# Expert stage of a Mamba-style mixer plus mixture-of-experts kernel: second weight ring filled only at a change of expert, row requests at other places, last small slot moved to the end

## The chip, the cores and the metric

The kernel runs on one core of a Trainium2 chip. The metric is the device time of one execution in microseconds; the median of three runs of the kernel before is 1149.23 us (1145.25 to 1150.15).

## The reference

The input is 4 sequences of 1024 tokens with 256 features (4096 tokens in all). Two layers follow each other.

```
x = x + layernorm(mixer(layernorm(x)))        # linear, conv, silu, selective scan, gated output
x = x + layernorm(ffn(layernorm(x)))

ffn:  probs = softmax(xn @ router_w)          # 8 experts
      topv, topi = top_k(probs, 2);  topv = topv / sum(topv)
      out = sum over e of comb[:, e] * (silu(clip(xn @ gate_e)) * (xn @ up_e)) @ down_e
          + shared expert
```

Each token goes to two of eight experts, so 8192 pairs of token and expert are computed, each expert with an inner width of 1024. With the reference's inputs the experts 0 to 7 get 508, 642, 476, 216, 1329, 3379, 439 and 1203 tokens.

## The kernel before

The first stage computes the mixer and, as tokens become ready, the routing; it also splits the experts' weights into a high and a low part and stores them in DRAM (`w_split`, `w_s` in the code: per expert 8 chunks of 768 KB, of which 512 KB are gate and up, 256 KB are down). Tokens are scattered to DRAM by expert (`xs_scratch`). This part ends at about 462 us.

The second stage (`experts`, from line 1231) works through 40 **slots**. A pair slot is 256 tokens of one expert in 8 steps; a small slot ("single") is 128 tokens in 4 steps. There are 31 pairs and 9 singles. `single(n)` (L1671) says which slots are small: 4, 8, ..., 36. Slots 0 to 4 are written out, slots 5 to 36 are a loop of eight iterations of four slots (`LEAD`, `BODY`, `REPEATS`, L51), slots 37 to 39 are written out again. Which expert a slot has is data: tables `group_expert`, `group_row`, `group_code`, `group_change`, filled by short vector instructions (L1062 to L1111 for the pairs; `plan_singles`, L1113, for the singles, one piece after each step of slot 0). The expert with the most tokens (5) comes first, with 13 pairs; the other pairs follow by expert number: 2, 3, 2, 1, 5, 2 and the 3 that still fit for expert 7. Singles are ordered by expert number too; an expert has one where its tiles of 128 tokens aren't covered by its pairs, and what is left over of the nine is an empty slot of expert 7.

TensorE multiplies each step's weights in three passes (high by high, high by low, low by high), VectorE and ScalarE make the activation, and 3 steps later (`LAG`) TensorE does the down product of that step. After a slot's last down product VectorE scales the result (`copy_y`, L1573; it stands at step 3 of the next slot), and GpSimd adds it to DRAM with one indirect transfer per 128 tokens (`add_y`, L1374; L1381). The adds of slot n wait until those of slot n-1 have landed (L1378).

SyncE (`sync`, L1284) issues all loads in one queue, in order:

- the **main ring** (`load_chunk`, L1300): 8 chunks, each in two transfers (L1302, L1303), conditional on `group_change`: where a pair has the same expert as the pair before, the instruction is there but moves nothing. A chunk's place is free when the slot before has done its down product with it (L1323).
- the **second ring** for the singles (`load_single`, L1305): 8 transfers of 768 KB, conditional too. They stand between the chunks in turns 4k+2 and 4k+3; a flag says which of the two turns issues them (the first one, where its main ring isn't reloaded; else the second). They are issued for each of the nine singles.
- the **rows** of the next slot (`next_rows`, L1285): 256 or 128 tokens, in a pair's turn after chunk 1 (L1325). It waits until the slot before has been weighed by VectorE (`meta_ready`, L1290; `weigh`, L1580, step 2 of a slot), since the buffer is that slot's.

The rows of slot 2 are asked for by the first line of `others` (L1351), after SyncE has waited for all scattered tokens and for padding rows that it writes behind each expert's tokens (L454 to L462).

At the end all adds must have landed (L1362), the sums are loaded, normalised and stored.

Of the kernel before, what the change touches and what calls it, by code (L numbers as in the profile page):

```python
# [4 lines left out]
F32 = mybir.dt.float32  # L5
F32R = mybir.dt.float32r
I32 = mybir.dt.int32
# [5 lines left out]
P = 128  # L13
# [34 lines left out]
NS = E + 1  # L48
NP = ((T * K + E * (P - 1)) // P - NS) // GT
SLOTS = NP + NS  # L50
LEAD, BODY, REPEATS = 5, 4, 8  # L51
CW = 4 * P + D
# [7 lines left out]
X_AT, D_AT, R_AT = 48, 48, 0  # L60
H_AT, XNT_AT, FULL_AT = 146080, 162496, 219456
GUW = 2 * 4 * P
# [3 lines left out]
def mixer(nc, x, w_e, w_s, weights, full, consts, shared, xs_dram, x1_dram, acc_dram, fill, vec, ident,  # L66
# [3 lines left out]
    with ExitStack() as ctx:  # L70
# [73 lines left out]
        unused, expert_f, passed_f, row_f, starred = [decay[:, 1, (4 + i) * 48:(4 + i) * 48 + NP] for i in range(5)]  # L144
        singles_at = [XNT_AT + k * 8 * CW for k in range(5)] + [H_AT + k * 8 * CW for k in range(2)] + [FULL_AT]
        single_ring = [nc.alloc_sbuf_tensor_at(f"single_ring{f}", [P, 2 * CW], F32R, offset=at) for f, at in enumerate(singles_at)]
        banks = [ctx.enter_context(nc.psum_tensor(f"bank{i}", [P, HALF], F32)) for i in range(8)]
# [45 lines left out]
        def free(engine, what):  # L193
# [17 lines left out]
            elif what == "acc":  # L211
                engine.wait_ge(ends_cleared, 16 * (E + 2))
                for i in range(2):
# [16 lines left out]
        x1 = [by_tile(flat(v[:, :, :])[:, k * TC * D:(k + 1) * TC * D]) for v in (e_raw, e_high) for k in range(2)]  # L230
        homes = (gu_ring, d_ring, single_ring, quad(u_flat[:, R_AT:R_AT + 2 * GT * ROW]), quad(x_home[0]), quad(x_home[1]),
                 u_flat[:, R_AT + 2 * GT * ROW:R_AT + 2 * GT * ROW + DC * G].rearrange("p (c g) -> p c g", g=G),
# [127 lines left out]
        def _(sp):  # L360
            rows_of_star, weights_of_star, other_groups = e_sync(sp)

# [22 lines left out]
            def store_shared(k):  # L385
                for f in range(2):
                    rows = slice(k * HALF + f * 2 * P, k * HALF + (f + 1) * 2 * P)
                    sp.wait_ge(s_out, 2 * k + f + 1)
                    sp.dma_start(acc_dram[rows, :].rearrange("(t p) d -> p t d", p=P), sh_of(k)[f]).then_inc(s_stored[buf_of(k)][f], 16)
# [65 lines left out]
            for e in range(E):  # L455
                row = sp.value_load(end_row[0:1, e:e + 1], min_val=e * CAP, max_val=e * CAP + T)
                sp.dma_start(xs_dram[bass.ds(row, G), :].rearrange("(p m) d -> p (m d)", p=P), spare).then_inc(ends_cleared, 16)
            store_shared(2 * B - 1)
            sp.wait_ge(ends_cleared, 16 * (E + 2))
            for half in range(2):  # L460
                sp.wait_ge(scattered[half], B * 16 * HT * K)
            sp.wait_ge(plan_ready, 1)  # L462
            other_groups()
# [338 lines left out]
        def _(dve):  # L802
# [261 lines left out]
            def planned(i):  # L1064

                n[0] += 1
                i.then_inc(steps, 1)
                dve.wait_ge(steps, n[0])
# [25 lines left out]
            thirds = expert_f[:, 0:3 * NS].rearrange("p (i k) -> p i k", k=3)  # L1094
            nc.vector.tensor_tensor(group_change[:, NP:SLOTS], thirds[:, :, 2], thirds[:, :, 1], ALU.is_equal)

# [16 lines left out]
            def plan_singles(step):  # L1113
# [28 lines left out]
                if step == 6:  # L1142
                    nc.vector.tensor_copy(group_expert[:, NP:SLOTS], code)
                    nc.vector.tensor_scalar(group_code[:, NP:SLOTS], code, -1.0, float(E), ALU.mult, ALU.add)
                    planned(nc.vector.scalar_tensor_tensor(out=row, in0=number[:, 0:NS], scalar=float(P), in1=row,
                                                        op0=ALU.mult, op1=ALU.add))
                    planned(nc.vector.tensor_scalar(rest, number[:, 0:NS], float(-P), float(SPARE), ALU.mult, ALU.add))
                if step == 7:
                    planned(nc.vector.tensor_tensor(rest, rest, ended[:, :, E - 1], ALU.mult))
                    planned(nc.vector.tensor_tensor(row, row, rest, ALU.add))  # L1150
                    nc.vector.tensor_copy(group_row[:, NP:SLOTS], row).then_inc(plan_ready, 1)
# [79 lines left out]
def experts(nc, ctx, w_s, xs_dram, acc_dram, x1_dram, out, group_expert, group_change, group_row, group_code, vec, ident, neg_half,  # L1231
# [12 lines left out]
    by_chunk = lambda v: v.rearrange("p (m c k) -> p c m k", m=2, c=DC)  # L1244
    gus_hi, gus_lo = [[by_chunk(v[:, at:at + 4 * P]) for v in w_single] for at in (0, CW)]
    ds_hi, ds_lo = [[v[:, at + 4 * P:at + CW] for v in w_single] for at in (0, CW)]
    ids = sb("ids", [P, 2, GT], I32)
# [36 lines left out]
    def sync(sp):  # L1284
# [19 lines left out]

        def load_single(f, e, wanted):  # L1305
            sp.dma_start(w_single[f][:, :].bitcast(F32), w_s[e, f, :, :], cond=wanted).then_inc(single_loaded, 16)

        def turn(i, n):
            if single(n):
                if n + 1 < SLOTS:  # L1310
                    next_rows(i, n)
                return
            e = sp.value_load(group_expert[0:1, bass.ds(table_at(i, n), 1)], min_val=0, max_val=E - 1)
            new = sp.value_load(group_change[0:1, bass.ds(table_at(i, n), 1)], min_val=0, max_val=1)
            last = n - 2 if single(n - 1) else n - 1
            to_come = NP + before(i, n, ones_at)
            loads_single = n % BODY in (2, 3) and n + 3 < SLOTS
            if loads_single:
                e_single = sp.value_load(group_expert[0:1, bass.ds(to_come, 1)], min_val=0, max_val=E - 1)
                flag = to_come if n % BODY == 2 else table_at(i, n - 1)  # L1320
                wanted = sp.value_load(group_change[0:1, bass.ds(flag, 1)], min_val=0, max_val=1)
            for f in range(FC):
                sp.wait_ge(down_done, before(i, last, steps_at) + f + 1 + FC)  # L1323
                load_chunk(f, e, new)
                if f == 1:  # L1325
                    next_rows(i, n)
                if loads_single:
                    if f == 0 and n > BODY:
                        sp.wait_ge(down_done, before(i, n - n % BODY, steps_at) + FC // 2 + FC)
                    load_single(f, e_single, wanted)  # L1330

# [12 lines left out]
        def others():  # L1344
# [5 lines left out]

            next_rows(0, 1)  # L1351
            free(sp, "x1")
# [17 lines left out]
            sp.wait_ge(out_added, 16 * (NC // 2))  # L1370
        return first_rows, first_weights, others

# [37 lines left out]
    def tensor(pe):  # L1410
# [26 lines left out]
        def gate_up_single(i, n, j):  # L1437
            par = n % 2
            if j == 0:
                pe.wait_ge(single_loaded, before(i, n, ones_at) * (32 * FC) + 32 * FC)  # L1440
                pe.wait_ge(x_lo_ready, before(i, n, one) * DC + DC)
# [229 lines left out]
def single(n):  # L1671

    return (0 < n < LEAD + BODY * REPEATS and n % BODY == 0)

# [42 lines left out]
def program(nc, d, out):  # L1717
# [5 lines left out]
    with ExitStack() as ctx:  # L1723
# [4 lines left out]
        group_expert = sb("group_expert", [P, SLOTS], I32)  # L1728
        group_change = sb("group_change", [P, SLOTS], I32)
        group_row = sb("group_row", [P, SLOTS], I32)  # L1730
# [3 lines left out]
        pad = sb("pad", [P, GT, ROW])  # L1734
        tables = [sb("start_row", [P, E]), sb("limits", [P, E, MAXG]), sb("number", [P, SLOTS])]
        fill = sb("fill", [P, E])
        ident = sb("ident", [P, P])
# [32 lines left out]
```

## Time and profile before

| what | value |
|---|---|
| median of 3 runs | 1149.23 us |
| profiled execution, its own time | 1156.33 us |
| profiled execution, span from first to last instruction | 1154.6 us |
| TensorE busy | 1041.0 us, 90% |
| VectorE, ScalarE, GpSimd busy | 69%, 54%, 25% |
| mean granted TensorE clock | 0.969 |
| bytes moved by DMA | 246.72 MB |

The profile page gives shares of the whole span. The stage that the change touches is the second one; there the order of time matters more than sums, and the chain of work that ended last, listed by time, shows where TensorE turned each slot's rows (L1419): the distances between these entries are the lengths of the slots.

### The profile page before, as it was taken

The page shows a single profiled execution, that of the slowest core. Times are in us where ns is not written, and L with a number is a line of the kernel's source. Part 1 is how long each engine was busy: PE and PEld are TensorE (multiplying, and loading weights), DVE is VectorE, ACT ScalarE, POOL GpSimd, SP SyncE. Part 2 cuts the span into 40 slices and gives each one's busy share as a digit, 9 for nine tenths or more (in the row PEclk, how much of TensorE's full clock was granted, in tenths as well). Part 3 has the DMA queues.
Part 4 walks back from the last instruction along what each step waited for, and adds up shares of the span by engine and source line. Part 5 has one row for each costly group of instructions (what it writes and reads, how often), then busy time and mean ns, then how long its engine had stood idle before and what let it go on. Part 6 is the DMA issues. An engine that isn't in the chain of part 4 may idle for free.

```text
span 1154.6 us, 22702 instructions
## 1 busy us (share of the span) xinstructions
PE 1041.0 (90%) x7042; PEld 917.3 (79%) x7042; DVE 800.8 (69%) x2051; ACT 623.7 (54%) x1269; POOL 287.1 (25%) x302
## 2 busy tenths in 40 slices
PE   4889999999988998899999999999998699998940
PEld 2666777677666655899999999999998699998940
DVE  5996899897879767566666666666665366665645
ACT  6768868777775364354544544344444244443415
POOL 1133032743252445021212112121121112111125
PEclk9999999999999999899999999999999999999975
DMA  8664766874675588872837264893939945398249
GB/s 305 210 219 168 261 204 223 299 248 146 220 237 188 200 287 300 283 270 65 283 76 235 39 209 128 301 359 76 374 91 330 352 118 164 100 351 263 57 94 216
DMA packets 130715, 246.72 MB, mean 214 GB/s; under 512 B 10848, under 2 KB 76128, under 8 KB 130656
## 3 DMA queue, kind: packets, MB, share of 16 engines
q1 hardware_dynamic: 115248, 226.08, 56.2%
q0 software_dynamic: 15408, 19.93, 9.6%
q8 instruction: 27, 0.44, 0.2%
q14 instruction: 32, 0.26, 0.1%
HBM read 357.61 MB, written 85.50 MB: 384 GB/s over the span
## 4 chain that ended last, share of the span: by engine, by line
PE 68%; DMA 8%; DVE 7%; SPq 7%; issue 4%; ACT 3%; POOL 2%; another core or an unknown queue 1%; DVEq 0%; ACTq 0%; POOLq 0%
PE bank L477 12%; PE bank L1432 8%; PE bank L1434 8%; PE bank L1433 8%; PE bank L1477 4%; PE bank L1479 4%; PE bank L1478 4%; PE bank L471 4%; PE bank L472 4%; PE bank L473 4%; DMA w_both<-w_split 3%; SPq L1302 2%; SPq L1303 1%; PE bank L1448 1%; PE bank L1450 1%
## 5 line engine op out<-in xcount | busy, mean ns | idle before, releaser
L1614 DVE TENSOR_SCALAR cv<-bank 128x256 f32<-128x256 f32 x284 | 120.3, 424 | 182.9 <-PE bank L1434 148.5
L1381 POOL DMA_INDIRECT acc_scratch<-cv,ids x71 | 111.1, 1564 | 541.9 <-DVE cv L1577 518.5
L1544 ACT ACTIVATE cv<-cv 128x256 f32<-128x256 f32 x284 | 118.4, 417 | 210.5 <-DVE cv L1614 207.3
L1432 PE MATMUL bank<-h_hi,w_both 128*128 128x256 f32 x744 | 209.8, 282 | 18.1 <-DMA w_both<-w_split 15.4
L1433 PE MATMUL bank<-h_hi,w_both 128*128 128x256 f32 x744 | 207.3, 279 | 0.0
L1434 PE MATMUL bank<-h_hi,w_both 128*128 128x256 f32 x744 | 207.3, 279 | 0.0
L1432 PEld LDWEIGHTS bank<-h_hi,w_both 128*128 128x128 f32 x744 | 141.0, 190 | 22.0 <-issue 10.5
L1530 ACT ACTIVATE h_lo<-cv 128x256 fp32r<-128x256 f32 x248 | 103.1, 416 | 88.3 <-DVE cv L1617 87.3
L1617 DVE TENSOR_TENSOR cv<-bank,cv 128x256 f32<-128x256 f32 x284 | 120.2, 423 | 41.0 <-ACT cv L1544 37.2
L1434 PEld LDWEIGHTS bank<-h_hi,w_both 128*128 128x128 f32 x744 | 140.9, 189 | 0.0
L1433 PEld LDWEIGHTS bank<-h_hi,w_both 128*128 128x128 f32 x744 | 140.9, 189 | 0.0
L471 PE MATMUL bank<-xs_hi,w_both 128*128 128x512 f32 x224 | 98.7, 441 | 21.1 <-DVE delta L859 8.6
L1477 PE MATMUL bank<-w_both,h_lo 128*128 128x256 f32 x372 | 104.1, 280 | 0.0
L1595 DVE TENSOR_TENSOR h_lo<-cv,h_lo 128x256 fp32r<-128x256 f32 x248 | 102.8, 415 | 0.8 <-ACT h_lo L1530 0.6
L1478 PE MATMUL bank<-w_both,h_lo 128*128 128x256 f32 x372 | 103.2, 277 | 0.0
L1479 PE MATMUL bank<-w_both,h_lo 128*128 128x256 f32 x372 | 103.1, 277 | 0.0
L472 PE MATMUL bank<-xs_lo,w_both 128*128 128x512 f32 x224 | 89.4, 399 | 0.0
L473 PE MATMUL bank<-xs_hi,w_both 128*128 128x512 f32 x224 | 89.2, 398 | 0.0
L1202 POOL DMA_INDIRECT xs_scratch<-n,slot_now x64 | 70.4, 1100 | 62.0 <-DVE slot_now L997 44.4
L1185 POOL TENSOR_TENSOR h_lo<-h,h_hi 128x512 fp32r<-128x512 f32 x32 | 49.2, 1542 | 107.7 <-ACT h_hi L731 107.6
L471 PEld LDWEIGHTS bank<-xs_hi,w_both 128*128 128x128 f32 x224 | 43.3, 193 | 39.0 <-issue 13.8
L1021 DVE TENSOR_TENSOR e_raw<-e_raw,e_high 128x768 f32<-128x768 f32 x64 | 65.7, 1028 | 10.0 <-ACT e_high L783 10.0
(268 smaller groups left out, 2653.8 us busy)
## 6 DMA issues: line engine op xcount, KB each, us to landing
single_ring<-w_split SPq DMA_DIRECT2D x144, 768.0 KB
w_both<-w_split SPq DMA_DIRECT2D x180, 512.0 KB
w_both<-w_split SPq DMA_DIRECT2D x180, 256.0 KB
e_raw<-w_e SPq DMA_DIRECT2D x64, 384.0 KB
w_split<-e_high SPq DMA_DIRECT2D x64, 384.0 KB
w_split<-e_raw SPq DMA_DIRECT2D x64, 384.0 KB
xs_hi<-w_split SPq DMA_DIRECT2D x30, 512.0 KB
xs_lo<-w_split SPq DMA_DIRECT2D x30, 512.0 KB
```

The source lines that it names most:

```text
L471: nc.tensor.matmul(out, hi, x_hi, start=first, stop=False)
L472: nc.tensor.matmul(out, hi, x_lo, start=False, stop=False)
L473: return nc.tensor.matmul(out, lo, x_hi, start=False, stop=last)
L477: return nc.tensor.matmul(out, w, x, start=first, stop=last)
L1432: nc.tensor.matmul(out, gu_hi[f][:, cols], xg_hi[:, par, c, :], start=c == 0, stop=False)
L1433: nc.tensor.matmul(out, gu_hi[f][:, cols], xg_lo[:, par, c, :], start=False, stop=False)
L1434: k = nc.tensor.matmul(out, gu_lo[f][:, cols], xg_hi[:, par, c, :], start=False, stop=c == DC - 1)
L1477: nc.tensor.matmul(out, hg_hi[:, f % 4, toks], d_hi[f], start=f == 0, stop=False)
L1478: nc.tensor.matmul(out, hg_hi[:, f % 4, toks], d_lo[f], start=False, stop=False)
L1479: k = nc.tensor.matmul(out, hg_lo[:, f % 4, toks], d_hi[f], start=False, stop=f == FC - 1)
L1614: nc.vector.tensor_scalar(half, gate_ps, CLIP, -CLIP, ALU.min, ALU.max).then_inc(clipped, 1)
L1617: nc.vector.tensor_tensor(half, up_ps, half, ALU.mult).then_inc(h_ready, 1)
```

## The change

In SyncE's turns the second ring is filled by three transfers (5 chunks, 2 chunks, 1 chunk) in place of eight, and only where a single's expert differs from that of the single before: a new table `fresh` is multiplied into the flag of turn 4k+2, and turn 4k+3 gets a flag of its own. A transfer whose flag is 0 is still an instruction in the queue. The rows of the next slot are requested after chunk 0, in place of chunk 1; in the turn after a single they are requested after the last chunk. The request for the rows of slot 2 is moved out of `others` to a place ahead of the waits for padding and scattered tokens. `REPEATS` goes from 8 to 7 and `single` counts the last slot in: singles are now 4, 8, ..., 32 and 39, and slots 33 to 38 are pairs, written out. Addresses of some buffers move by 256 bytes, since a table has grown.

```diff
-LEAD, BODY, REPEATS = 5, 4, 8
+LEAD, BODY, REPEATS = 5, 4, 7
...
-        singles_at = [XNT_AT + k * 8 * CW for k in range(5)] + [H_AT + k * 8 * CW for k in range(2)] + [FULL_AT]
-        single_ring = [nc.alloc_sbuf_tensor_at(f"single_ring{f}", [P, 2 * CW], F32R, offset=at) for f, at in enumerate(singles_at)]
+        steady, fresh = [decay[:, 1, (9 + i) * 48:(9 + i) * 48 + NS] for i in range(2)]
+        single_ring = [nc.alloc_sbuf_tensor_at(f"single_ring{at}", [P, places, 2 * CW], F32R, offset=at)
+                       for at, places in ((XNT_AT, 5), (H_AT, 2), (FULL_AT, 1))]
...
             store_shared(2 * B - 1)
+            sp.wait_ge(plan_ready, 1)
+            third_rows()
             sp.wait_ge(ends_cleared, 16 * (E + 2))
             for half in range(2):
                 sp.wait_ge(scattered[half], B * 16 * HT * K)
-            sp.wait_ge(plan_ready, 1)
             other_groups()
...
-            nc.vector.tensor_tensor(group_change[:, NP:SLOTS], thirds[:, :, 2], thirds[:, :, 1], ALU.is_equal)
+            nc.vector.tensor_tensor(steady[:, :], thirds[:, :, 2], thirds[:, :, 1], ALU.is_equal)
...
                 if step == 6:
...
+                    nc.vector.memset(fresh[:, 0:1], 1.0)
+                    planned(nc.vector.tensor_tensor(fresh[:, 1:NS], code[:, 1:NS], code[:, 0:NS - 1], ALU.not_equal))
...
                 if step == 7:
...
+                    planned(nc.vector.tensor_tensor(steady[:, :], steady[:, :], fresh[:, :], ALU.mult))
+                    nc.vector.tensor_copy(group_change[:, NP:SLOTS], steady[:, :])
+                    nc.vector.tensor_tensor(group_change[:, SLOTS:SLOTS + NS], fresh[:, :], steady[:, :], ALU.subtract)
...
-        def load_single(f, e, wanted):
-            sp.dma_start(w_single[f][:, :].bitcast(F32), w_s[e, f, :, :], cond=wanted).then_inc(single_loaded, 16)
+        def load_singles(part, e, wanted):
+            first = sum(v.shape[1] for v in w_single[0:part])
+            to = w_single[part].bitcast(F32)
+            sp.dma_start(to, w_s[e, first:first + to.shape[1], :, :].rearrange("f p c -> p f c"), cond=wanted).then_inc(single_loaded, 16)
...
-                flag = to_come if n % BODY == 2 else table_at(i, n - 1)
+                flag = to_come + (0 if n % BODY == 2 else NS)
...
                 load_chunk(f, e, new)
-                if f == 1:
+                if f == (FC - 1 if single(n - 1) else 0):
                     next_rows(i, n)
-                if loads_single:
+                if loads_single and f < len(w_single):
                     if f == 0 and n > BODY:
                         sp.wait_ge(down_done, before(i, n - n % BODY, steps_at) + FC // 2 + FC)
-                    load_single(f, e_single, wanted)
+                    load_singles(f, e_single, wanted)
...
-            next_rows(0, 1)
             free(sp, "x1")
...
-                pe.wait_ge(single_loaded, before(i, n, ones_at) * (32 * FC) + 32 * FC)
+                pe.wait_ge(single_loaded, before(i, n, ones_at) * (32 * len(w_single)) + 32 * len(w_single))
...
-    return (0 < n < LEAD + BODY * REPEATS and n % BODY == 0)
+    return n == SLOTS - 1 or (0 < n < LEAD + BODY * REPEATS and n % BODY == 0)
```

## Rows read from the trace of the kernel before

**Rows 1.** The page, part 1: busy time of each engine, its share, instructions.

```profile
PE 1041.0 (90%) x7042; PEld 917.3 (79%) x7042; DVE 800.8 (69%) x2051; ACT 623.7 (54%) x1269; POOL 287.1 (25%) x302
```

**Rows 2.** Waits, whole span: waiter, what it waited for, us, times, longest.

```profile
PE bank L1432 <- DMA w_both<-w_split: 15.4, 11, 3.1
...
PE bank L1419 <- DMA u<-xs_scratch: 2.7, 1, 2.7
...
PE bank L1448 <- DMA single_ring<-w_split: 1.0, 1, 1.0
```

**Rows 3.** The chain by time, 560 to 1160 us: start, us, what; turns of slots.

```profile
597.21 0.44 PE bank L1419 x4
...
625.94 0.44 PE bank L1419 x4
...
717.52 0.44 PE bank L1419 x4
...
782.81 0.44 PE bank L1419 x4
...
845.14 0.44 PE bank L1419 x4
...
923.13 0.44 PE bank L1419 x4
...
1045.21 0.44 PE bank L1419 x4
...
1077.86 0.44 PE bank L1419 x4
```

**Rows 4.** The chain by time, 480 to 640 us: first turns of the stage.

```profile
482.84 2.69 DMA u<-xs_scratch
...
505.42 0.44 PE bank L1419 x4
...
522.22 0.22 PE bank L1419 x2
```

**Rows 5.** Windows: busy per engine, granted clock, DMA share, GB/s (last three).

```profile
1003.00:1022.00 19.00, 18.71 (x165) 18.52 (x164) 12.03 (x34) 8.99 (x22) 2.55 (x2) 1.00 1.03 343
...
1033.00:1041.00 8.00, 8.00 (x73) 8.00 (x72) 5.78 (x19) 4.12 (x11) 3.10 (x2) 1.00 1.02 425
...
485.00:490.00 5.00, 4.43 (x21) 4.43 (x22) 0.00 (x0) 0.00 (x0) 0.00 (x0) 0.50 0.31 104
```

**Rows 6.** SyncE's instructions by time in turn 34: start, us, line, what.

```profile
1008.99 0.54 SPq L1302 DMA_DIRECT2D w_both<-w_split  x1
...
1010.63 0.08 SPq L1306 DMA_DIRECT2D single_ring<-w_split  x1
1011.05 0.54 SPq L1302 DMA_DIRECT2D w_both<-w_split  x1
```

**Rows 7.** SyncE's own waits, whole span: columns as in rows 2.

```profile
SPq L1290 <- DVE share L1590: 93.6, 9, 13.8
```

**Rows 8.** SyncE's instructions by time: the request of slot 10's rows, behind single 8.

```profile
603.82 0.39 SPq L1291 DMA_DIRECT2D u<-xs_scratch  x1
```

**Rows 9.** SyncE's instructions by time, ahead of the request of slot 2's rows.

```profile
477.62 0.98 SPq L389 DMA_DIRECT2D acc_scratch<-x_in  x2
```

**Rows 10.** VectorE by time: last instruction of the singles' plan.

```profile
480.47 0.17 DVE L1151 CAST group_row<-decay 128x9 int32<-128x9 f32 x1
```

**Rows 11.** VectorE by time: last step of slot 8 (a single) and of slot 39.

```profile
604.24 0.42 DVE L1614 TENSOR_SCALAR cv<-bank 128x256 f32<-128x256 f32 x1 [0.28 <-PE bank L1450]
...
605.54 0.86 DVE L1577 TENSOR_SCALAR cv<-bank,share 128x256 f32<-128x256 f32 x2
...
1106.99 0.42 DVE L1614 TENSOR_SCALAR cv<-bank 128x256 f32<-128x256 f32 x1 [0.71 <-PE bank L1434]
```

**Rows 12.** The chain by time at the end of the stage: the last add.

```profile
1113.84 3.79 DMA acc_scratch<-cv,ids
```

**Rows 13.** GpSimd by time: the second add of slot 7.

```profile
609.12 1.55 POOL L1381 DMA_INDIRECT acc_scratch<-cv,ids  x1 [0.30 <-issue]
```

More of the change, by code:

```diff
@@ L60 @@
 X_AT, D_AT, R_AT = 48, 48, 0
-H_AT, XNT_AT, FULL_AT = 146080, 162496, 219456
+H_AT, XNT_AT, FULL_AT = 146336, 162752, 219712
 GUW = 2 * 4 * P
@@ L230, in mixer @@
         x1 = [by_tile(flat(v[:, :, :])[:, k * TC * D:(k + 1) * TC * D]) for v in (e_raw, e_high) for k in range(2)]
-        homes = (gu_ring, d_ring, single_ring, quad(u_flat[:, R_AT:R_AT + 2 * GT * ROW]), quad(x_home[0]), quad(x_home[1]),
+        homes = (gu_ring, d_ring, [v[:, :, :] for v in single_ring], quad(u_flat[:, R_AT:R_AT + 2 * GT * ROW]), quad(x_home[0]), quad(x_home[1]),
                  u_flat[:, R_AT + 2 * GT * ROW:R_AT + 2 * GT * ROW + DC * G].rearrange("p (c g) -> p c g", g=G),
@@ L360, in _ @@
         def _(sp):
-            rows_of_star, weights_of_star, other_groups = e_sync(sp)
+            rows_of_star, weights_of_star, third_rows, other_groups = e_sync(sp)
             def load_x(b, half):
@@ L1244, in experts @@
     by_chunk = lambda v: v.rearrange("p (m c k) -> p c m k", m=2, c=DC)
-    gus_hi, gus_lo = [[by_chunk(v[:, at:at + 4 * P]) for v in w_single] for at in (0, CW)]
-    ds_hi, ds_lo = [[v[:, at + 4 * P:at + CW] for v in w_single] for at in (0, CW)]
+    places = [v[:, k, :] for v in w_single for k in range(v.shape[1])]
+    gus_hi, gus_lo = [[by_chunk(v[:, at:at + 4 * P]) for v in places] for at in (0, CW)]
+    ds_hi, ds_lo = [[v[:, at + 4 * P:at + CW] for v in places] for at in (0, CW)]
     ids = sb("ids", [P, 2, GT], I32)
@@ L1370, in others @@
             sp.wait_ge(out_added, 16 * (NC // 2))
-        return first_rows, first_weights, others
+        return first_rows, first_weights, lambda: next_rows(0, 1), others
     def gpsimd(pool):
@@ L1728, in program @@
         group_expert = sb("group_expert", [P, SLOTS], I32)
-        group_change = sb("group_change", [P, SLOTS], I32)
+        group_change = sb("group_change", [P, SLOTS + NS], I32)
         group_row = sb("group_row", [P, SLOTS], I32)
@@ L1735, in program @@
         tables = [sb("start_row", [P, E]), sb("limits", [P, E, MAXG]), sb("number", [P, SLOTS])]
+        sb("apart", [P, 3 * LT * 2])
         fill = sb("fill", [P, E])
```

## The prediction

> **What bounds the kernel now.** I read the page first: TensorE is busy for 90% of the span [rows 1], so the question is what lies in the remaining tenth and at a lower clock. The waits say that within the expert stage TensorE's idle time comes after transfers: the main ring's chunks, the rows of one slot, once the second ring [rows 2]. A sum of idle time hides what follows a wait, so I measure whole slots by the chain, between turns of rows. From single 8 at 597.21 to single 16 at 717.52, two periods of three pairs and a single, no wait shows: 60.16 us per period. Against that, the next periods took 65.29, 62.33 and 77.99, and the two up to 1045.21 together 122.08 [rows 3]. The losses are 5.13, 2.17, 17.83 and 1.76 us. From single 36 to the turn in slot 37 it is 32.65 against a regular 28.73 (597.21 to 625.94): 3.92 more. Together **30.8 us** are lost after 717 us, where experts change (reloads of the main ring in turns 17, 19, 23, 26, 27, 34, 37; 768 KB in 8 chunks, 6.29 MB each), and nearly none before, where one expert fills 13 pairs.
>
> A last piece stands at the start. The rows of slot 2 were requested at 482.84 and landed 2.69 us later [rows 4]; TensorE was idle for 2.7 of it [rows 2]. After that its granted clock was 0.50, the 1.2 GHz level, in 485 to 490 [rows 5], and from the turn that ended this wait (485.53) to the next at 505.42 it took 19.9 us, against 16.80 for an ordinary pair (505.42 to 522.22) [rows 4]. So one late request cost 2.7 + 3.1 = **5.8 us**.
>
> **The change part by part.**
>
> *Second ring.* With the token counts of the reference, expert 4 has 11 tiles and 5 pairs, so one single; expert 5 has 27 and 13, one; expert 7 has 10 tiles but 3 pairs are left for it, so four; the last three are empty slots of expert 7. The singles' experts are 4, 5, 7, 7, 7, 7, 7, 7, 7. Three of nine differ from the one before, those in slots 4, 8 and 12, so 6 × 6.29 = 38 MB of transfers go, all of them in the part where reloads are. The three that stay are in the quiet part; a fill of 6.29 MB takes 14.8 us at the 425 GB/s of the window in which only the second ring was filled [rows 5], less than the pair's 16.8 and a pair more ahead of its use, so nothing there is on the path.
>
> Of SyncE's time: a reloaded chunk takes 1.64 us of issue (1008.99 to 1010.63) and the skipped second-ring instruction behind it 0.42 more (to 1011.05) [rows 6]. That is 2.06 per chunk, against 16.8 / 8 = 2.10 that a step of TensorE takes: SyncE could not catch up once it was late. With three instructions in place of eight it gains 5 × 0.42 = 2.1 us per such turn.
>
> What is left of each reload then? Turn 34 is the nearest row: its chunks were loaded with nothing else in the queue, and the two periods around it lost 1.76, of which 1.0 was the wait for the second ring, which goes [rows 2, 3]. So a reload alone costs between 0 and 0.76; I take 0.4, since SyncE becomes quicker. That holds for turns 19, 23, 34, and for the reload of pair 28, which moves from slot 37 to slot 36, behind a pair. Four times 0.4 are 1.6 us.
>
> Turns 26 and 27 are the hard case: two reloads in a row, and before also a fill of the second ring in turn 27, three times 6.29 MB in about three slots. The fill goes. What stays are two reloads of 19 us each at 343 GB/s [rows 5] in two pair slots of 16.8 and a lead of several steps that the first chunk has. By these rows the excess is between nothing (the lead takes it) and 2 × 2.2 = 4.4; nearest is the low part, since the window of 19 us was paced by SyncE's 2.06 per chunk as well. I take 1.4.
>
> *Rows behind a single.* SyncE waited 93.6 us in 9 waits, 13.8 at most, for the weighing of the slot before [rows 7]: in the turn after a single it stood at L1290 with chunks 2 to 7 behind it. Where that turn has a reload (17 and 37) six chunks were issued late. With the request behind the last chunk, the chunks go out as their places come free; what is queued behind the request's wait is now the next turn only. The rows themselves are asked for some 0.6 us later than now: behind single 8 the request stood at 603.82 [rows 8], and two skipped instructions and the table's read come between. At 604.4 plus 2.69 [rows 4] they land at 607.1; they are turned at about 609.1 (597.21 + 28.73 - 16.80 [rows 3, 4]), so this is covered, by 2 us. With a reload in front of them (turn 17) it may be less; I take nothing and keep 1 us. Turn 17 then loses nothing, and the 3.92 at slot 37 fall to the 0.4 already counted.
>
> So of 30.8 us there remain 1.6 + 1.4 = 3.0, and **27.8** are gained (bounds 20 and 30.8).
>
> *Rows of slot 2.* The last stores ahead of the new place are issued by 478.60 [rows 9]; with the table read the request goes out at about 479.4, 3.4 us earlier, and lands 2.69 later at 482.1, or about 483 where it queues behind those stores. TensorE got there at 482.8. The five added vector instructions of the plan are like the one of 0.17 us [rows 10]; up to 0.6 us in slot 0, where TensorE hangs on VectorE, I take 0.3. Of 5.8 us **5.3** go (bounds 2 and 5.8).
>
> *The last slot.* Before, the last clip began at 1106.99 and the last add landed at 1113.84 + 3.79 = 1117.63 [rows 11, 12]: 10.64 us. A single at the end has only 4 steps, and the copy of the pair before it stands in the last of them. In slot 8 that copy began 1.30 after the same clip (604.24, 605.54) and the second add of that pair began at 609.12, 4.88 after the clip [rows 11, 13]. Its landing takes 3.79 [rows 12]; only then may the last single's add start (L1378), 0 to 0.85 us later (as the first add of slot 7 stood 0.87 behind the end of its copy: 609.12 less 1.85, less 606.40), and lands 3.79 later: 12.5 to 13.3. Two small transposes fall behind the clip instead of ahead, which gives back 0.4. The tail becomes longer by **2.2** (bounds 1.4 and 2.7). The one add less is not seen, since two landings now follow each other.
>
> *The sum:* 27.8 + 5.3 - 2.2 = **30.9 us** less. The profiled execution took 1156.33 (span 1154.6): 1125.4. The median of the runs is 1149.23, 0.6% below; with the same ratio (0.9733) this is **1118.5 us**. Loads and addresses else stay as they are: a shift of 256 bytes and a loop with one iteration less I cost at nothing.
>
> **The rivals.**
>
> *The reload itself is the bound.* If the 19.0 us of a reload [rows 5] come from the transfers and not from SyncE, each of the six reloads behind a pair (19, 23, 26, 27, 34, 36) keeps 2.2 us: 13.2 in place of 3.0, 1135.6 in the profile, **1128.6** as median. For it: DMA share 1.03 in that window. Against: turn 34 lost under 0.8, and 425 GB/s were reached 11 us later. By the Trainium skill, "DMA: Bandwidth & Descriptors", Specifications, a core has about 358 GB/s of HBM; an estimate from that is 17.6 us per reload and about 1121 for the median, and the trace disagrees as far as 425 goes above it. Chance 0.14.
>
> *The early request gains nothing*, because it lands behind the stores of 478 us and padding, all in one queue: the start keeps its 5.8, **1123.8**. The padding's landing is what the old place waited for. Chance 0.08.
>
> *The change doesn't do what it says:* singles are not skipped (the order of singles is not as I worked it out). Then a fill is one request of 3.93 MB and one of 1.57 MB right behind chunk 0 of a turn; in turn 27 the reload's chunk 1 stands behind 9.2 us of transfers at 425 GB/s [rows 5], where before 0.77 MB stood there, and in turns 18 and 22 the rest of the fill stands before the reloads of 19 and 23. Three times 9 us, half the clock behind each idle time as at 485 us (3 us each), and the tail's 2.2 are 38; the start and turns 17 and 37 give back 12: 26 more, **1175**. It decides from six differing singles on, if they include those of slots 20, 24 and 28. The counts say three. Chance 0.05, a part of which (0.02) ends near no change.
>
> **How the numbers follow.** Forecast 0.73, rivals 0.14, 0.08, 0.05. The best case (no remainder, start wholly gained, tail 1.4) is 35.2 less, 1114; three runs before lay within 5 us, so the low end is 1111. The high end takes in the first rival and 2 us more: 1131. A difference of 0.5% is about what a measurement of this kernel can tell from no change. Faster 0.95, within 0.5% 0.02, slower 0.03.
>
> **What would show it.** In the profile after, periods from single to single all near 60.2; no fills of the second ring after slot 10 (issues of under 0.15 us in its line); bytes moved down by about 38 MB; no clock of 0.50 near 485; the longest idle time left in slot 27; between the last clip and the last landing about 12.9 us. The prediction is wrong if slots 26 and 27 still lose over 5 us, or if TensorE's step of 2.10 us itself grows.

## The result

The changed kernel took 1134.27 us (median of 4 runs, 1131.14 to 1135.84) against 1149.69 for the kernel before in the same series: a ratio of 0.987 (0.983 to 0.990). A second series gave 1133.63 and 0.986 (0.983 to 0.988). So it is faster by 15 to 16 us, half of the 30.9 forecast, and 1134 lies outside the range of 1111 to 1131. The profiled execution of the changed kernel took 1135.84 (span 1134.1).

The page's first part, and the waits of the whole span (waiter, what it waited for, us, times, longest), of the changed kernel:

```profile
PE 1037.7 (91%) x7042; PEld 915.2 (81%) x7042; DVE 802.1 (71%) x2056; ACT 623.9 (55%) x1269; POOL 286.0 (25%) x302
```

```profile
PE bank L1441 <- DMA w_both<-w_split: 4.4, 4, 2.1
...
PE bank L1428 <- DMA u<-xs_scratch: 2.8, 1, 2.8
```

L1441 is the old L1432, L1428 the old L1419. The waits for chunks fell from 15.4 us to 4.4 (from 18.5 to 4.9 with chunks 6 and 7, which the profile lists under the names `xs_hi` and `xs_lo`), those for the second ring are gone, and one wait for rows of 2.8 us is there as before, but it is another one: then for the rows of slot 2 [rows 2], now for those of slot 18, in slot 17. The chain by time (start, us, what), turns of rows in slots 8, 16, 20, 24, 28, 32, 36 and 37:

```profile
593.58 0.44 PE bank L1428 x4
...
713.89 0.44 PE bank L1428 x4
...
781.44 0.44 PE bank L1428 x4
...
843.97 0.44 PE bank L1428 x4
...
905.99 0.44 PE bank L1428 x4
...
966.14 0.44 PE bank L1428 x4
...
1028.58 0.44 PE bank L1428 x4
...
1046.43 0.44 PE bank L1428 x4
```

Two undisturbed periods take 120.31 (593.58 to 713.89), as before. The next ones take 67.55, 62.53, 62.02 and 60.15: losses of 7.4, 2.4, 1.9 and 0 against 60.16, where the kernel before had 5.1, 2.2 and 17.8 [rows 3]. From slot 36 to 37 it is 17.85 against 16.82. The great loss of slots 26 and 27 is gone, and the first period became worse, not better.

Every slot can be set against its regular length in this way. Slot n runs from the turn that stands in it to the next one; regular lengths are 11.66 for a single, 17.07 for the pair behind it, 16.82 for the next pair and 14.61 for the last one ahead of a single, 60.16 in all. The losses in us, for two executions of each kernel:

| slots | before | before, again | forecast | changed | changed, again |
|---|---|---|---|---|---|
| 1 (rows of slot 2) | 6.1 | 1.6 | 0.5 | 0.1 | 0.0 |
| 16, 17 | 2.8 | 3.0 | 0 | 3.0 | 6.3 |
| 18, 19 | 2.3 | 1.5 | 0.4 | 4.4 | 2.8 |
| 22, 23 | 2.2 | 2.0 | 0.4 | 2.4 | 1.8 |
| 26, 27 | 17.9 | 17.9 | 1.4 | 1.9 | 2.0 |
| 33 to 35 | 1.8 | 0.7 | 0.4 | 0.1 | 0.2 |
| 36, 37 | 3.9 | 4.1 | 0.4 | 1.0 | 1.5 |
| last clip to last landing | 10.6 | 10.6 | 12.9 | 13.2 | 13.1 |

The time until TensorE turns slot 1's rows (in slot 0) varies from run to run: it is 465.4 and 465.8 us in the two executions before, 468.0 and 466.6 in the two after. So kernels with one profile are compared below by their **stage time**, from that turn to the end of the span: 689.2 and 683.0 before, 666.1 and 668.3 changed. (Two of the expectations call it the turn of slot 2's rows; their figures are counted from slot 1's.) The table's first line is counted from that turn too, against 16.9 us to the next one. From slot 16 on the losses are 30.8 and 29.1 us before, 12.7 and 15.0 changed.

### The profile page after: what moved, and what is told of

Its sections match the earlier page's. It is cut to its first block, busy times and chain, and to the rows that moved or that the text cites. A ratio compares the mean times of both kernels' runs of the same rounds, so it can differ in the third digit from the quotient of the medians.

```text
span 1134.1 us, 22278 instructions
## 1 busy us (share of the span) xinstructions
PE 1037.7 (91%) x7042; PEld 915.2 (81%) x7042; DVE 802.1 (71%) x2056; ACT 623.9 (55%) x1269; POOL 286.0 (25%) x302
## 2 busy tenths in 40 slices
DMA packets 123297, 208.78 MB, mean 184 GB/s; under 512 B 9824, under 2 KB 74848, under 8 KB 123232
## 4 chain that ended last, share of the span: by engine, by line
PE 77%; DVE 7%; DMA 6%; issue 3%; POOL 2%; ACT 2%; SPq 2%; ACTq 0%; DVEq 0%; POOLq 0%
PE bank L479 14%; PE bank L1441 9%; PE bank L1443 9%; PE bank L1442 9%; PE bank L1488 5%; PE bank L1486 5%; PE bank L1487 5%; PE bank L473 4%; PE bank L474 4%; PE bank L475 4%; PE bank L1459 1%; PE bank L1457 1%; PE bank L1458 1%; DMA w_both<-w_split 1%; PE bank L1428 1%
## 5 line engine op out<-in xcount | busy, mean ns | idle before, releaser
L1441 PE MATMUL bank<-h_hi,w_both 128*128 128x256 f32 x744 | 208.0, 280 | 5.3 <-DMA w_both<-w_split 4.4
L1441 PEld LDWEIGHTS bank<-h_hi,w_both 128*128 128x128 f32 x744 | 140.4, 189 | 7.0 <-issue 5.0
L473 PE MATMUL bank<-xs_hi,w_both 128*128 128x512 f32 x224 | 100.0, 447 | 20.5 <-DVE delta L861 10.2
L475 PE MATMUL bank<-xs_hi,w_both 128*128 128x512 f32 x224 | 90.4, 403 | 0.0
L473 PEld LDWEIGHTS bank<-xs_hi,w_both 128*128 128x128 f32 x224 | 44.0, 197 | 38.7 <-DVE delta L861 15.4
```

Of the source, the lines that this page charges most:

```text
L473: nc.tensor.matmul(out, hi, x_hi, start=first, stop=False)
L475: return nc.tensor.matmul(out, lo, x_hi, start=False, stop=last)
L1441: nc.tensor.matmul(out, gu_hi[f][:, cols], xg_hi[:, par, c, :], start=c == 0, stop=False)
```

## The experiments

Two theories of what is left stand against each other in several expectations. The *order theory* says that a transfer is late because SyncE issues it late, behind other instructions; the *transfer theory* says that it is late because of the bytes that move ahead of it.

**The kernel before, again** (no edit).

> The kernel before once more, unchanged. If the profile that the forecast was read from was an ordinary one, the slots after 717 us lose 30.8 us again, within 2 us, most of it (17.8) in turns 26 and 27, and the 6.6 us by which that profile lay above the median are in the first stage. If that profile was a dear one in the expert stage, turns 26 and 27 lose clearly less here, say 10 to 12, and the whole stage some 24: then the forecast started from about 6 us that most runs of the kernel before don't have.

1150.59 us, stage 683.0. The chain by time at the start of the stage, and the window (busy per engine, granted clock, DMA share, GB/s last):

```profile
479.78 4.43 DMA u<-xs_scratch
484.26 0.66 PE bank L1419 x4
501.28 0.44 PE bank L1419 x4
```

```profile
485.00:490.00 5.00, 5.00 (x46) 5.00 (x45) 2.28 (x9) 2.05 (x5) 0.00 (x0) 1.00 0.00 1
```

Here the rows were asked for at 479.78, not at 482.84 [rows 4]; TensorE waited 1.5 us, not 2.7, and the clock behind that stayed at 1.00, where the forecast's profile shows 0.50, the 1.2 GHz level [rows 5]. The start lost 1.6 us, not 6. Turns 26 and 27 lost 17.9 again. So neither alternative of the expectation holds as written: the losses after 717 us were ordinary (29.1 against 30.8), the first stage was as long (465.8 against 465.4), and what was particular to the profile that the forecast used was the start.

**The row request of slot 2 back at its old place.**

```
             store_shared(2 * B - 1)
-            sp.wait_ge(plan_ready, 1)
-            third_rows()
             sp.wait_ge(ends_cleared, 16 * (E + 2))
...
+            sp.wait_ge(plan_ready, 1)
+            third_rows()
             other_groups()
```

> The changed kernel with one part undone: the rows of slot 2 are requested where they were, behind the waits for padding and scattered tokens. Theory: the idle time of 2.7 us and the half clock behind it come back, slot 1 takes 5.8 to 6.0 us more, time 1140. Rival: the changed kernel's profile reached the first expert slot 2.6 us later than that of the kernel before; if the early request is what made the first stage longer, only about 3 us are lost by undoing it, time 1137.

1133.84 us (1130.67 to 1135.79), ratio 0.987 (0.983 to 0.992): no change against 1134.27. The stage time is 666.0, that of the changed kernel; slot 1 loses 0.5 us. Both theories fall: the late request costs little in most executions. In the four profiles that have it (this one, the two of the kernel before, and that with the skip alone, below) it cost 0.5, 6.1, 1.6 and 0.5 us. Counted from the turn of slot 1's rows, the request went out after 14.6, 17.4, 14.0 and 14.5 us there, and after 11.4 in the changed kernel: only one of the four was very late.

**Fills for all nine singles.**

```
-                    planned(nc.vector.tensor_tensor(fresh[:, 1:NS], code[:, 1:NS], code[:, 0:NS - 1], ALU.not_equal))
+                    planned(nc.vector.tensor_tensor(fresh[:, 1:NS], code[:, 1:NS], code[:, 1:NS], ALU.is_equal))
```

> The changed kernel with the second ring filled for each of the nine singles again (three transfers each), all else as changed; 38 MB more are moved. Theory: the fill in turn 27 stands between the chunks of its reload, 3.9 MB right behind chunk 0, so turns 26 and 27 lose 14 to 18 us in place of 1.9; turns 18 and 22 have the fill right ahead of a reload and lose 2 more each; turn 35 some 1 to 2; time 1152 to 1158. Rival, the reload alone is the bound and fills hide beside the pairs that have no reload: only turn 27 pays, 6.3 MB at 400 GB/s less one pair's slack, 8 to 10 us, time 1143.

1149.57 us, ratio to the kernel before 1.000 (0.998 to 1.002); stage 686.1. Slots 26 and 27 lose 16.4, 33 to 35 lose 7.0; 18, 19, 22 and 23 pay nothing for the fill ahead of them (1.8 and 2.0). SyncE's instructions by time in turn 27 (start, us, line, what), and the wait that follows in the chain:

```profile
879.46 0.38 SPq L1316 DMA_DIRECT2D single_ring<-w_split  x1
880.19 0.56 SPq L1310 DMA_DIRECT2D w_both<-w_split  x1
...
881.85 0.38 SPq L1316 DMA_DIRECT2D single_ring<-w_split  x1
882.57 3.03 SPq L1310 DMA_DIRECT2D w_both<-w_split  x1
885.88 3.41 SPq L1311 DMA_DIRECT2D w_both<-w_split  x1
```

```profile
885.88 14.24 DMA w_both<-w_split
```

3.9 and 1.6 MB stand between the chunks, and chunk 2's second transfer lands 14 us after its issue. With all nine fills made, all other parts of the change together thus left the time where it was.

**The skip alone,** in the kernel before: eight transfers, rows after chunk 1, late request, last single at 36.

```
-                flag = to_come if n % BODY == 2 else table_at(i, n - 1)
+                flag = to_come + (0 if n % BODY == 2 else NS)
...
+                    planned(nc.vector.tensor_tensor(fresh[:, 1:NS], code[:, 1:NS], code[:, 0:NS - 1], ALU.not_equal))
```

> The kernel before with the skip alone: the second ring filled only where its expert changes, still in eight transfers beside the chunks, rows after chunk 1, row request of slot 2 and last small slot as before. With everything but the skip the time was that of the kernel before (ratio 0.9998). Theory, the skip is the whole gain and the other parts cancel out: turns 26 and 27 lose 2 to 4 in place of 17.9, turns 18, 19, 22, 23 about 1 each less, turns 17 and 37 keep 3.1 and 4.2: 1134 to 1135. Rival, the skip needs the other parts, since eight skipped instructions of 0.42 us each still hold SyncE up beside each reloaded chunk (2.06 us per chunk against a step of 2.04 to 2.10): turns 26 and 27 keep 6 to 8 us, time 1140.

1136.19 us, ratio 0.989 (0.987 to 0.992), stage 668.6: about 13 of the 16 us. Slots 26 and 27 lose 4.9, 36 and 37 4.7, 16 and 17 2.9: between the theory and its rival, in time nearer to the theory. The intervals of this ratio and of the changed kernel's overlap, so the 2 us that the other parts add are not clear of the noise.

**The last small slot at 36 again.**

```
-LEAD, BODY, REPEATS = 5, 4, 7
+LEAD, BODY, REPEATS = 5, 4, 8
...
-    return n == SLOTS - 1 or (0 < n < LEAD + BODY * REPEATS and n % BODY == 0)
+    return (0 < n < LEAD + BODY * REPEATS and n % BODY == 0)
```

> The changed kernel with the last small slot at 36 again, all else as changed. Theory: from the last clip to the landing of the last add 10.6 us in place of 13.2; slot 36 no longer waits for its last chunk (1.0 us less); but turn 37 is now a reload behind a single, with its row request behind all eight chunks, as turn 17, and loses 3.0 as that does: 0.6 us less in all, time 1133.7. Rival, the late rows of turn 17 have another cause than their place behind the reload: turn 37 loses nothing and the time is 3.6 less, 1130.7.

1137.19 us, stage 670.3. Slots 36 and 37 lose 7.1 in place of 1.0: a wait of 3.6 for rows and the rest at a granted clock of 0.50 behind it. That is the mechanism of turn 17 a second time, at a higher price than the 3.0 that I gave it, and it outweighs the shorter tail. With the rows behind the last chunk, the move of the last single is what keeps the reload of pair 28 cheap.

**Rows behind a single requested after chunk 4.**

```
-                if f == (FC - 1 if single(n - 1) else 0):
+                if f == (FC // 2 if single(n - 1) else 0):
```

> The changed kernel, but in a turn behind a single the rows are requested after chunk 4 in place of chunk 7. What is compared is the time from the turn of slot 2's rows (slot 1) and the loss of slots 16 and 17 against regular ones, which was 3.0 + 0.3 us in the changed kernel and 3.0 + 1.9, 3.5 + 1.9 in two relatives. Order theory: the rows come late because they stand behind the whole reload; weighed at about 720.5, requested at once, with only chunks 0 to 4 ahead, they land in time and slots 16 and 17 lose under 0.5; chunks 5 to 7, held back until then, still have over 10 us. Transfer theory: the rows share the DMA queues with the reload whatever their place, and the loss stays at 3 or more, or moves to chunks 5 to 7 of slot 17.

1130.12 us, stage 664.9. No wait for rows is left; but slots 16 and 17 still lose 2.4, now all in slot 17. VectorE by time shows the wait behind it:

```profile
728.57 0.22 DVE L1595 SCALAR_TENSOR_TENSOR part<-u,group_code 128x2 f32<-128x2 f32 x1 [3.50 <-DMA acc_scratch<-cv,ids]
```

Weighing slot 17 waits until the adds of slot 15 have landed, since it writes their index table; these adds were requested at 719.36 and 721.22, among the last chunks of the reload, and slot 17's clip stands behind the weighing. That the reload is what delays them is argued, not shown. This wait is not new; the kernel before had it in the same turn (3.95 us, up to 737.51) and in turn 37 (4.33), beside its waits for chunks. Its waits, whole span:

```profile
DVE part L1586 <- DMA acc_scratch<-cv,ids: 10.0, 4, 4.3
```

The order theory is right on the rows; what was gained there went in part to the adds. In the three profiles with rows after chunk 4 (two follow below) slot 16 loses 0.0, in the seven with rows after chunk 7 and full reloads 3.0 to 3.7. The 1.2 us of stage time alone would not show it: that is less than two executions of the changed kernel differ by.

**Rows after chunk 1 behind a pair.**

```
-                if f == (FC - 1 if single(n - 1) else 0):
+                if f == (FC - 1 if single(n - 1) else 1):
```

> The changed kernel, but in a pair's turn behind a pair the rows are requested after chunk 1, where the kernel before has them, in place of chunk 0. Losses now: slots 18 and 19 together 2.2 to 4.4 us, 22 and 23 1.7 to 2.4, 26 and 27 1.9 to 2.3, each time waiting for chunk 1. Order theory: chunk 1 is issued 1.4 us earlier in turns 19, 23 and 27, so these three lose 1.4 us less each, and what follows at half clock goes too: 4 to 6 us less in all. Transfer theory: the bytes ahead are the same and chunk 2 or the rows are late in its place: within 1 us of now.

1150.26 us, stage 681.8: in slots 18 to 23 3.1 lost in place of 6.8 and 4.6, and 17.1 us lost where neither theory looked, in slots 1, 2, 5, 6, 9 and 10. SyncE in turn 6, and the landing of its rows in the chain:

```profile
557.35 0.39 SPq L1316 DMA_DIRECT2D single_ring<-w_split  x1
...
559.91 0.39 SPq L1299 DMA_DIRECT2D u<-xs_scratch  x1
```

```profile
559.91 10.79 DMA u<-xs_scratch
```

The rows stand behind the 3.9 MB of the second ring's first transfer and land after 10.79 us in place of 2.69 [rows 4]. So rows after chunk 0 and three large transfers go together: whoever makes eight transfers into three must put the rows ahead of them. By the Trainium skill, "DMA: Bandwidth & Descriptors", Queues, rings and completion order, each DMA engine takes the descriptors of one issuing engine's queue in their order; this row agrees with that.

**Tables read a turn ahead.** SyncE reads expert and flags of turn n+1 beside chunk 4 of turn n, where both are pairs.

```
+                if f == 4 and n % BODY in (1, 2):
+                    known[n + 1] = tables(i, n + 1)
...
+            e, new, e_single, wanted = known.pop(n) if n in known else tables(i, n)
```

> The changed kernel, but SyncE reads the tables for a turn (expert, flags) in the turn before it, beside chunk 4, where both slots are pairs; the order of the transfers is as in the changed kernel. Chunk 0 of turn 19 went out at 752.6, some 1.7 us after its place was free, because of four table reads ahead of it. Order theory: chunks 0 and 1 go out 1.5 us earlier or more in turns 19, 23 and 27, their waits of 2.1, 1.4 and 0.6 us become 0.5, 0 and 0, 3 to 5 us less in all. Transfer theory: chunk 1 lands when the queues have moved rows, adds and chunk 0, whatever the issue: less than 1 us gained.

Stage 662.8, 3.3 us less than the changed kernel (its time of 1122.79 also has a first stage that was 10 us shorter, ending at 458.2). SyncE in turn 19 of the changed kernel, then the landing that TensorE waited for in the chain:

```profile
752.62 0.60 SPq L1310 DMA_DIRECT2D w_both<-w_split  x1
753.50 0.56 SPq L1311 DMA_DIRECT2D w_both<-w_split  x1
755.06 0.37 SPq L1299 DMA_DIRECT2D u<-xs_scratch  x1
755.73 0.07 SPq L1316 DMA_DIRECT2D single_ring<-w_split  x1
756.14 0.56 SPq L1310 DMA_DIRECT2D w_both<-w_split  x1
756.98 0.55 SPq L1311 DMA_DIRECT2D w_both<-w_split  x1
```

```profile
756.98 6.09 DMA w_both<-w_split
```

and with the tables read ahead:

```profile
739.72 0.12 SPq L1310 DMA_DIRECT2D xs_lo<-w_split  x1
...
741.77 0.58 SPq L1310 DMA_DIRECT2D w_both<-w_split  x1
...
745.27 0.55 SPq L1310 DMA_DIRECT2D w_both<-w_split  x1
```

From chunk 0 to chunk 1 it is 3.5 us in both (row request, its table read, a skipped fill); but the whole turn starts 1.5 us earlier (here 2.05 us after the last chunk of turn 18; there, with that chunk at 749.10, 3.52). Slots 18, 19, 22 and 23 lose 0.8 in all in place of 6.8 and 4.6. This is a single run, but the three profiles with tables read ahead (two follow) lose 0.3 to 1.0 there, and the six without them, with rows after chunk 0 and full reloads, 3.8 to 6.8. So the isolated reloads were late by SyncE's order, by its table reads above all. Slots 26 and 27, two reloads in a row, lose 3.4 and did not gain.

**All of SyncE's order changed at once.**

```
+                if f == (FC // 2 if single(n - 1) else 1):
...
+                if loads_single and f >= FC - len(w_single):
...
+                    known[n + 1] = tables(i, n + 1)
```

> The changed kernel with all of SyncE's order mended: rows after chunk 1 behind a pair and after chunk 4 behind a single, tables read a turn ahead, the second ring's three instructions beside chunks 5 to 7 in place of 0 to 2. Order theory: of the 12.8 us that slots 16 to 36 lose in the changed kernel only the two reloads in a row (26 and 27, 1 to 2 us) and the last chunk of turn 36 (0.5 to 1) stay; 10 us less, time 1124. Transfer theory: only the wait of slot 16 for its rows goes, the reloads behind pairs keep 7 to 9 us in all, time 1131.

1149.68 us, ratio 1.001 (0.998 to 1.004); the profile is of the fastest of its ten executions, with a stage of 681.4. Slots 18 to 23 lose 0.3, as the order theory says; but with the second ring's transfers beside chunks 5 to 7 the rows of the next turn stand behind them, and slots 2, 3, 6, 7, 10 and 11 lose 22 us. It is the fault of the rows after chunk 1 once more, at another place.

**Half of each reload left out.**

```
-            sp.dma_start(halves(w_gu[f]), gu, cond=new).then_inc(loaded[f], 16)
+            sp.dma_start(halves(w_gu[f])[:, :, 0:2 * P], gu[:, :, 0:2 * P], cond=new).then_inc(loaded[f], 16)
```

(and the same for the down part)

> The changed kernel with half the columns of each reloaded chunk left out (gate, up and down parts; what stays in the ring there are the weights of the expert before): the same instructions at the same places, 3.15 in place of 6.29 MB per reload. Transfer theory for what is left: slots 26 and 36 lose nothing, the rows of slot 18 land within 3 us of their request (request at 8 us ahead of the end of the reload no longer behind a backlog), 18 and 22 lose nothing: all losses of slots 16 to 36 under 2 us of 12.8. Order theory: chunk 1 of turns 19 and 23 is still issued 3.5 us behind chunk 0 and 4.8 ahead of its need, so some wait of it stays, 0.5 to 1 us each, and slot 16 still waits for rows requested at 722, some 0.5.

1120.28 us, stage 654.7. All that is left of TensorE's waits for transfers in the expert stage:

```profile
PE bank L1441 <- DMA w_both<-w_split: 0.4, 1, 0.4
```

Slots 16 and 17 lose 0.0, 18 and 19 0.3, 22 and 23 0.1, 26 and 27 0.7, 36 and 37 nothing. With SyncE's order unchanged, fewer bytes take nearly all of it away. So both theories hold: chunk 1 of turn 19 in the changed kernel was issued at 756.14 and needed at 761.1 (TensorE's wait of 2.11 us ended at 763.19), a lead of 4.9 us; it is late if its landing takes longer, and an earlier issue helps as well as fewer bytes.

**The changed kernel again, and the two mends that helped, together** (tables a turn ahead; rows behind a single after chunk 4).

> The changed kernel once more, unchanged, as the measure for the three beside it: 1134, stage time from the turn of slot 2's rows to the end 666.1 us, losses of slots 16 to 36 between 12.5 and 15 us with the same places (16 and 17, 18 and 19, 22 and 23, 26, 36). If instead the losses change place or size by more than 3 us, single profiles can't carry the comparison of orders.

> The changed kernel with tables read a turn ahead and, behind a single, rows requested after chunk 4. Order theory: the two gains add up (3.3 and 1.2 us of stage time against the changed kernel), slots 18 to 23 lose under 1, slots 16 and 17 about 2.5, slot 26 keeps 3: stage 661.5, time 1129.5, ratio to the kernel before 0.983. Transfer theory: what is issued earlier only waits longer in the queues, and adds and rows behind it are later: stage 664 to 666, time 1132 to 1134.

The changed kernel: 1133.63 us, ratio 0.986 (0.983 to 0.988), stage 668.3; sizes vary (slots 16 and 17 lost 6.3, 18 and 19 2.8), places don't. The 3.3 us more in slots 16 and 17 are over the 3 us that the expectation set, so a difference of 1 or 2 us between two single profiles shows nothing; what several profiles have in common does. Both mends: **1127.30 us**, ratio 0.983 (0.980 to 0.986), stage 662.1. Slots 16 and 17 lose 2.0, 18 to 23 1.0, 26 and 27 3.4. That is 6.3 us (0.6%) below the changed kernel in the medians of one series, and 4.0 and 6.2 in stage time; the intervals of the two ratios overlap a little.

## Why the prediction was wrong

The sum was 27.8 + 5.3 - 2.2 = 30.9. In the two profiles that it was made for, the span fell by 20.5, in the medians the time fell by 15 to 16. The first term missed most: the losses from slot 16 on fell by 18.1 in these two profiles and by 14.1 in the second two, where 27.8 were forecast. The start gave 6.0 and 1.6 for 5.3, the tail cost 2.6 and 2.5 for 2.2. (The rest to 20.5: a first stage 2.6 longer, and 1.6 gained by the other order of slots and behind the last landing.)

**The skip: right.** Three of nine singles are filled, and the page has 208.78 MB moved, 38 less than before. Slots 26 and 27 lose 1.9 and 2.0, forecast 1.4, of 17.9. This is the gain: alone it brings 13 us, and without it the rest brings nothing. The third rival (no skip, 1175) had the mechanism right in turn 27 but was 25 us too dear: fills ahead of the reloads of 19 and 23 cost nothing.

**The start: a term of 5.3 us that most executions don't have.** The late request cost 0.5, 0.5, 1.6 and 6.1 us in four profiles. I read it from one execution and had the sign before me: that execution lay 7.1 us above the median. I scaled the sum by 0.6% instead of asking which rows carried the excess; the start was most of it (4.5 us more than in the second profile). In the changed kernel the request did go out early (at 479.47, forecast 479.4), the clock in 485 to 490 is 1.00, as forecast; there was just little to gain:

```profile
485.00:490.00 5.00, 5.00 (x46) 5.00 (x45) 2.89 (x10) 2.47 (x6) 0.00 (x0) 1.00 0.11 40
```

**"What is left of each reload", 0.4 us each: mis-sized for turns 19, 23 and 36,** 2.8 to 4.4, 1.8 to 2.4 and 1.0 to 1.5. I took turn 34 as the nearest row, and slots 33 to 35 did lose only 0.1 to 0.2. But it was not a near row. SyncE in the changed kernel ahead of turn 34's chunk 0, and its wait in 974 to 984:

```profile
972.37 0.12 SPq L1311 DMA_DIRECT2D xs_lo<-w_split  x1
...
983.60 0.61 SPq L1310 DMA_DIRECT2D w_both<-w_split  x1
```

```profile
SPq L1310 <- PE bank L1488: 7.4, 1, 7.4
```

Turn 33, behind a single, had its places free early, so SyncE had read the four tables of turn 34 by 975.9 and stood waiting for the place of chunk 0. That chunk went out 5.95 us after TensorE's turn in slot 33 (977.65). In turn 19 the four reads (749.68 to 752.2) begin only behind the last chunk of turn 18, chunk 0's place is free when they end, and it goes out 7.15 us after the turn in slot 18 (745.47). With the tables read ahead it is 5.68. In the kernel before it was 5.96 and 7.55, so the difference stood in the trace that I forecast from.

I also counted the five skipped instructions that went and not the request that came: in turns 19 and 23 it was moved ahead of chunk 1, and I gave that no price at all. It costs 1.4 us of SyncE (754.06, the end of chunk 0's second instruction, to 755.43) and puts 256 rows ahead of chunk 1, which lands 6.09 us after its second instruction. How much of the loss this is stays open: with tables not read ahead and full reloads, slots 18 to 23 lose 3.8 to 6.8 with the request there (six profiles) and 3.1 to 4.5 with it behind chunk 1 (four). Reading the tables a turn ahead takes 3.8 to 6.0 us away.

**"Turn 17 then loses nothing": failed by its own step.** I had the rows land at 607.1 in slot 8, 2 us ahead of their need, and kept 1 us for a reload ahead of them. SyncE and the chain in the changed kernel:

```profile
720.52 0.55 SPq L1311 DMA_DIRECT2D xs_lo<-w_split  x1
722.14 0.40 SPq L1299 DMA_DIRECT2D u<-xs_scratch  x1
```

```profile
722.14 6.08 DMA u<-xs_scratch
728.35 0.65 PE bank L1428 x4
```

SyncE's old wait of 93.6 us [rows 7] is gone, the chunks go out in time; but the rows land 6.08 us after their request. Most chunks are issued faster (every 1.7 us, the last two 2.2) than they move (an estimate: 786 KB at the 398 GB/s below take 1.98 us), so the queue still holds some of them; with half of the bytes slot 16 loses 0.0. The window of the changed kernel in which they move (columns as above):

```profile
716.00:726.00 10.00, 9.55 (x82) 9.35 (x80) 6.61 (x19) 3.40 (x9) 1.75 (x2) 1.00 1.06 398
```

In the kernel before slot 17 lost 2.8, with a wait of 1.1 us for chunk 4 and VectorE's wait for the adds beside it; now slot 16 loses 3.0 by the rows. Halving the bytes or an earlier place removes this; at the earlier place the adds are next, which the forecast had left out. The longest idle time of TensorE's slots, forecast for slot 27, is this one.

**Pair 28's reload and the tail: right in kind.** The reload costs 1.0 to 1.5 in slots 36 and 37 where 3.9 to 4.1 were lost. The tail by VectorE and the chain:

```profile
1084.42 0.42 DVE L1623 TENSOR_SCALAR cv<-bank 128x256 f32<-128x256 f32 x1 [0.64 <-PE bank L1459]
```

```profile
1089.25 3.82 DMA acc_scratch<-cv,ids
...
1093.83 3.82 DMA acc_scratch<-cv,ids
```

From the last clip to the last landing (1097.65) it is 13.2 us, forecast 12.5 to 13.3; before, 10.6 [rows 11, 12]. Two landings follow each other, as foreseen.

**The rivals.** The first one (each reload is bound by its transfers, 2.2 us each) gave 1128.6 and was the nearest. Its sizes fit 19 and 23 by chance: in 26, 27 and 34 a reload lost about 1 or less, and in the isolated turns the order decided. The second one (nothing gained at the start) came true in its size, though not by its queue. I had priced each alone; both at once, by the forecast's own terms, give 1133.9. That this meets the measured time is luck: the rival has 2.2 us for each of six reloads and nothing for turn 17, the profiles have 3.0 to 6.3 in slots 16 and 17 and 0.1 to 0.2 in 33 to 35. By the Trainium skill, "DMA: Bandwidth & Descriptors", Latency and other measured facts, HBM answers later under load (0.2 us on average, 2 us at high load); here only the sum is seen, rows of 2.69 us alone and 6.08 behind a reload, and no run splits that into queue and latency.

**Two readings.** The window 1033 to 1041 [rows 5] holds not only a fill of the second ring: rows are requested in it at 1036.12 and the first chunks of turn 37 from 1038.10 on, so 425 GB/s is the rate of all three. And the 16.80 us that I took for the pair behind single 8 is the length of another pair; that one takes 17.07, so slot 10's rows were turned at 608.9, not 609.1. Neither changes the sum.

## What to carry to other kernels

Before a wait seen in one execution goes into a sum, ask whether that execution is an ordinary one: where its time lies above the median, look for the rows that carry the excess, and give them a low end near nothing. Before a row is taken as the nearest one, ask whether the issuing engine stood waiting there and hid work that is on the path elsewhere. In a queue that one engine issues in order, every moved request is a price for what is now behind it, in issue time and in bytes, and the size of the transfers decides which order is possible: the rows must stand before a fill of 3.9 MB, though they then stand before the chunk that is needed first, too. Here the transfers that need not be made were worth more than all reordering around them.

## What was not expected of the hardware

The granted clock behind a wait of about 3 us differs between executions of the same kernel. Windows behind the wait for the rows of slot 18, of the changed kernel and of its second profile (columns as above):

```profile
728.00:731.00 3.00, 2.65 (x23) 2.66 (x24) 1.09 (x3) 1.19 (x4) 0.00 (x0) 1.00 0.38 52
```

```profile
727.00:730.00 3.00, 2.43 (x12) 2.44 (x13) 0.44 (x2) 0.86 (x3) 0.00 (x0) 0.50 0.20 31
730.00:733.00 3.00, 3.00 (x16) 3.00 (x16) 0.67 (x3) 0.55 (x2) 0.00 (x0) 0.50 0.00 0
```

After 2.80 us of idle time TensorE went on at 1.00, the 2.4 GHz level, and slot 17 lost 0.05; after 3.57 us it ran at 0.50, the 1.2 GHz level, for about 5 us and slot 17 lost 2.6. But the kernel with the row request of slot 2 at its old place waited 2.83 us here, fell to 0.50 and lost 1.6 in slot 17, while that with tables read ahead waited 3.34 us, stayed at 1.00 and lost 0.05. So the length of the wait alone does not tell which.

SyncE's transfer instruction itself, mostly 0.55 us, took 3.0 to 3.4 us in turn 27 of the kernel that fills for all singles, where fills of 5.5 MB had been issued in the 3 us before. No wait for a semaphore is shown there; that what SyncE has already issued holds it up is likely, but no run tests it.
